# Loads in channel layout and stores as 128-partition transfers of 256 KB, in a fused transformer block on one NeuronCore

## The reference

```
x = x + conv_attention(ln_over_channels(x))      # q, k, v by 64x64 weights, 8 heads,
                                                 # softmax over an 8x8 score per head, Wout, bias
t = x as tokens (1024 x 64)
t = t + layer_norm(moe(ln(t)) + ln(t)) * gamma + beta
    # moe: routing weights from the mean token of an image, the best 2 of 8 experts,
    # each gelu(t W1 + b1) W2 + b2 with a hidden width of 128
out = t back as channels
```

## Time and profile before

| | us |
|---|---|
| median of 3 runs | 103.39 (103.19 to 103.40) |
| the profiled execution | 103.3 |
| its span, first to last instruction | 101.5 |
| TensorE busy | 86.3 |
| VectorE busy | 66.8 |
| ScalarE busy | 50.4 |
| GpSimd busy | 32.5 |

### The profile page before, as it was taken

One profiled execution on the slowest core, in us unless ns is written; L12 is line 12 of the kernel. 1 busy time (PEld: TensorE's weight loads), 2 busy tenths in 40 slices (PEclk: granted clock), 3 DMA queues, 4 the chain that ended last, 5 costly groups with the idle time before them and its releaser, 6 DMA issues.

```text
span 101.5 us, 2245 instructions
## 1 busy us (share of the span) xinstructions
PE 86.3 (85%) x748; PEld 45.9 (45%) x749; DVE 66.8 (66%) x235; ACT 50.4 (50%) x88; POOL 32.5 (32%) x82
## 2 busy tenths in 40 slices
PE   4997999997999978999869996899999999985200
PEld 1344796896751544699322272323423333341100
DVE  0098998964488998699999527261752726677920
ACT  0000765735666121138578998968877792510000
POOL 7000000008000000044380999472805601960500
PEclk9999999999999999999999999999999999999655
DMA  2999999800000000024200436830000260075075
GB/s 53 287 405 299 287 275 347 217 5 0 0 6 0 0 0 3 6 52 103 52 0 20 96 93 151 201 72 0 6 0 0 65 141 6 0 178 132 0 166 144
DMA packets 6554, 9.82 MB, mean 97 GB/s; under 512 B 1040, under 2 KB 3344, under 8 KB 6544
## 3 DMA queue, kind: packets, MB, share of 16 engines
q1 hardware_dynamic: 4848, 6.77, 25.4%
q10 hardware_dynamic: 1696, 2.92, 10.2%
HBM read 5.49 MB, written 2.10 MB: 75 GB/s over the span
## 4 chain that ended last, share of the span: by engine, by line
PE 69%; DVE 9%; DMA 7%; ACT 4%; issue 4%; ACTq 1%; DVEq 1%
PE pC L1221 14%; DMA cst<-consts_dram 7%; PE pB L917 4%; PE pS L917 4%; PE pA L927 4%; PE pA L1196 3%; PE pB L1196 3%; PE pM L1032 2%; PE pA L990 2%; PE pM L1004 2%; ACT SQ L433 2%; PE pC L1213 2%; PE pS L1066 2%; PE pC L978 2%; PE pS L978 2%
## 5 line engine op out<-in xcount | busy, mean ns | idle before, releaser
L1221 PE MATMUL pC<-H,w2g 128*64 128x512 f32 x64 | 15.8, 602 | 0.0
L484 POOL TENSOR_TENSOR LO<-UF,HI 128x512 f16<-128x512 f32 x8 | 9.2, 1159 | 20.4 <-ACT HI L344 19.5
L610 DVE BATCH_NORM_STATS2 bst<-XT 128x6 f32<-128x128 f32 x32 | 6.5, 282 | 4.9 <-DMA XT<-x_tok_dram 4.9
L1111 PE MATMUL pM<-wz 128*128 128x512 bf16 x25 | 8.0, 491 | 1.3 <-POOL wz L477 1.3
L238 POOL TENSOR_TENSOR XT<-XT,T 128x512 f32<-128x512 f32 x6 | 7.5, 1270 | 4.0 <-DVE XT L879 4.0
L420 ACT ACTIVATE H<-pA,b1s 128x1024 f32<-128x1024 f32 x6 | 6.7, 1111 | 2.5 <-PE pA L1196 2.3
L500 POOL COPY w1g<-w1hl 128x256 f16 x14 | 5.1, 402 | 8.1 <-issue 6.0
L344 ACT CAST HI<-UF 128x512 f16<-128x512 f32 x8 | 4.8, 618 | 5.1 <-DVE UF L718 5.1
L433 ACT ACTIVATE SQ<-pC,c 128x512 f32<-128x512 f32 x8 | 5.4, 686 | 3.8 <-PE pC L1221 3.0
L490 POOL TENSOR_TENSOR w1hl<-SQ,w1hl 128x512 f16<-128x512 f32 x2 | 2.3, 1156 | 15.2 <-DVE A L657 15.2
L855 DVE TENSOR_SCALAR U<-pC,c,wsm 128x512 f32<-128x512 f32 x8 | 6.2, 800 | 1.4 <-PE pC L1221 0.9
(11 more groups left out here) (230 smaller groups left out, 185.8 us busy)
## 6 DMA issues: line engine op xcount, KB each, us to landing
out_dram<-XT SPq DMA_DIRECT2D x14, 128.0 KB, 2.4
XT<-x_tok_dram SPq DMA_DIRECT2D x2, 512.0 KB, 8.9
X<-x_cha_dram SPq DMA_DIRECT2D x8, 128.0 KB, 11.0
X<-x_cha_dram ACTq DMA_DIRECT2D x8, 128.0 KB, 11.1
ST<-HI SPq DMA_DIRECT2D x6, 128.0 KB, 2.4
ST<-LO SPq DMA_DIRECT2D x6, 128.0 KB, 2.4
XT<-x_tok_dram SPq DMA_DIRECT2D x2, 256.0 KB, 4.6
XT<-x_tok_dram ACTq DMA_DIRECT2D x2, 256.0 KB, 4.8
```

Source lines behind the costliest of these rows:

```text
L484: nc.gpsimd.tensor_tensor(LO[:, p, cols], UF[:, p, cols], HI[:, p, cols], ALU.subtract).then_inc(s["lo"], 1)
L610: return nc.vector.bn_stats(bst[:, p, j, :], XT[:, p, j * P:(j + 1) * P].rearrange("p (b c) -> p c b", b=2))
L1111: mm(pM[:, :], wz[:, 0:P], wz[:, :], start=True, stop=True)
L1221: last = mm(half(y_ps[:, b * HALF:(b + 1) * HALF], h), w2g[:, p % 2, b, k, :], H[:, step % 2, b, h * HALF:(h + 1) * HALF], start=False, st ...
```

## The change

The loads of X and the stores of OUT now take both halves h of an image at once: one transfer of 128 partitions and 256 KB where there were two of 64 partitions and 128 KB. SP loads image 0 of each pair and ACT image 1. SP stores seven images, ACT the very last one; the store waits for one s_fin only. Each s_x[p] and s_out[p] now ends at 32. TensorE waits for cstb (s_cstb) before the experts' first products. No arithmetic is changed.

```
+        def both_halves(ap):
+            return ap.rearrange("c (h n) -> h c n", h=2)
+        def load_x(queue, p, b):
+            queue.dma_start(X[:, p, b * HALF:(b + 1) * HALF],
+                            both_halves(x_cha[b * C:(b + 1) * C, p, :])).then_inc(s_x[p], 16)
+        def store(queue, p, b):
+            queue.wait_ge(s_fin[2 * p + b], 1)
+            queue.dma_start(both_halves(out[b * C:(b + 1) * C, p, :]),
+                            OUT[:, p, b * HALF:(b + 1) * HALF]).then_inc(s_out[p], 16)
...
             for p in range(NP):
-                for b in range(2):
-                    sp.dma_start(X[0:C, p, b * HALF:(b + 1) * HALF],
-                                 x_cha[b * C:(b + 1) * C, p, 0:HALF]).then_inc(s_x[p], 16)
+                load_x(sp, p, 0)
...
             for p in range(NP):
-                for b in range(2):
-                    sp.wait_ge(s_fin[2 * p + b], 1)
-                    for h in range(2 if p < NP - 1 else 1):
-                        sp.dma_start(out[b * C:(b + 1) * C, p, h * HALF:(h + 1) * HALF],
-                                     OUT[h * C:(h + 1) * C, p, b * HALF:(b + 1) * HALF]).then_inc(s_out[p], 16)
+                for b in range(2 if p < NP - 1 else 1):
+                    store(sp, p, b)
             for p in range(NP):
-                sp.wait_ge(s_out[p], 64)
+                sp.wait_ge(s_out[p], 32)
...
             for p in range(NP):
-                for b in range(2):
-                    act.dma_start(X[C:P, p, b * HALF:(b + 1) * HALF],
-                                  x_cha[b * C:(b + 1) * C, p, HALF:N]).then_inc(s_x[p], 16)
+                load_x(act, p, 1)
...
-            for b in range(2):
-                act.wait_ge(s_fin[2 * NP - 2 + b], 1)
-                act.dma_start(out[b * C:(b + 1) * C, NP - 1, HALF:N],
-                              OUT[C:P, NP - 1, b * HALF:(b + 1) * HALF]).then_inc(s_out[NP - 1], 16)
+            store(act, NP - 1, 1)
...
-                dve.wait_ge(s_x[p], 64)
+                dve.wait_ge(s_x[p], 32)
...
             pe.wait_ge(s["w1h"], 2)
             pe.wait_ge(s["w1l"], 2)
+            pe.wait_ge(s_cstb, 16)
```

## The result

The changed kernel takes 149.87 us (median of 4 runs, 148.37 to 152.06), the kernel before 103.4 on the same chip. The ratio is 1.4364, with a 95% interval of 1.4326 to 1.4403. That is slower, by 45 us of 103, and inside the predicted range. The kernel was profiled twice. The profiled executions took 151.33 and 148.64 us, with spans of 149.5 and 146.8. Some executions take about 2% longer than the others, the first profiled one among them, and the ratio is that of the shorter ones (148.4 to 148.7 us).

The account below looks back on a forecast made before the run. Bound by TensorE and the VectorE and ScalarE steps it waits for, transfers only at the ends. Span 101.5 + 23.2 + 2.4 + 23.6 = 150.7, plus 1.8 and 0.1 gives 152.6 us; range 144 to 176.

Parts of the forecast that it names:

- Two engines: Changed X loads and stores: DRAM side 2x64x512 is dealt out by its first dimension, to two DMA engines instead of sixteen.
- Rival 1: Changed transfers: pattern is flattened, all sixteen engines carry them, the last store lands earlier; 102.3 us, chance 10%.
- The speed: Changed transfers: each DMA engine moves 24 GB/s, so 5.46 us a transfer; ends 25.9 and 14.9 to 16.3.
- rival 3: Changed transfers: two engines, packets as slow as in 64-partition rows; 200 us, some 176 with half that slowing; over 176: 8%.
- Term 1: X loads: last image pair lands at 56.3 us, so VectorE's last residual additions and everything behind move by +23.2 us.
- Rival 2: ScalarE's X issues: two engines, full queue holds ScalarE until 45.4; +34.6 in place of +23.2, 164.0 us, chance 13%.
- Term 2: TensorE after some 20 us waiting for X: restarts at the lower clock, +2.4 us, range 0 to 4.
- Term 3: Stores at the end: eight transfers of 5.46 us on the same two engines, one always waiting; +23.6 us.

## Why the prediction held, step by step

**Two engines: right.** The share of 0.12 at 48 GB/s that it named stands in both plateaus, at 0.13 and 50 to 51 GB/s (about 49 in the page's slices). With 16 and with 128 rows in front the share is 1.04, with four 0.27, so the engines follow the first dimension. Rival 1 (sixteen engines after all) is out for the changed kernel. As a statement on the kernel with 128 rows in front it was close, 102.3 against 101.6.

On the rule that the prediction had named for it (the Trainium skill, DMA: Bandwidth & Descriptors, section Why a DMA increments its semaphore by 16 and not by 1: the largest number up to 16 that divides the slowest dimension of both sides) the traces agree in all four cases: 2, 4, 16 and 16 engines.

**The speed: close.** Taken were 24 GB/s an engine and 5.46 us a transfer. The closing stretch of the second profile gives 51/2 = 25.5 GB/s for the stores, so 5.1 us. For the loads, the version with all of them on SP's queue shows a pair (two transfers) every 10.7 us, so 5.34 us a transfer and 24.5 GB/s an engine. The slow end of the range, 14.9 to 16.3, can be dropped for two engines, and with it rival 3.

**Term 1, the loads, +23.2: the size is right, the account of it only half.** Measured are +23.3 (33.13 to 56.44), and X is what released the last addition. The pairs' arrivals came out as well: 34.5, 45.4 and 56.3 were forecast, and VectorE read them at 35.0, 45.7 and 56.4 where nothing else held it. But the wait of some 20 us that VectorE was to have there is 1.49 and 2.45 in the two profiles. The delay had mostly come earlier, since ScalarE was held. Rival 2 had named that mechanism, and had set its end at 45.4, where the third of its transfers would have moved. The end was 32.6. The chain of waits of the second profile shows it (start, duration, what):

```profile
5.74 1.08 ACTq L239
6.85 3.69 ACTq L239
10.57 11.47 ACTq L239
22.07 34.29 DMA X<-x_cha_dram
```

The third issue takes 11.47 us and the fourth, from 22.07 to 32.60, 10.5, each about the 10.9 of a pair of transfers. They end at 22.1 and 32.6, just ahead of the 23.5 and 34.5 that the prediction gave for the first and second pair. So ScalarE's fourth issue ended with the second pair, not with the third, and the hold stayed 1.5 us short of deciding. That was in part luck: the forecast had left the hold out and given it to rival 2, and the hold happened to be just shorter than the delay of X itself. Both delays sat side by side, and the version without the hold showed that X alone makes all of term 1.

**Term 2, TensorE gone cold, +2.4: wrong in the shorter runs, and misplaced.** TensorE's long idle time lay at 20 to 40 us under the held ScalarE (4.96 us busy, clock 0.51), not ahead of the last pair. It cost almost nothing there: from ScalarE's first work to VectorE's addition of the first pair it is 50.29 - 32.60 = 17.7 us, against 28.29 - 10.83 = 17.5 before. By 40 to 55 us the clock was at 0.97 again. The price that was forecast does appear where the wait falls directly ahead of dense work: +2.5 in the first profile (clock 0.55 from 59 to 66) and +3.0 with all loads on SP's queue (0.50 from 57 to 66). So the size was about right where it was paid, and whether it was paid depended on the hold that term 1 had not counted. That the size fits is in part luck: it was taken from eleven weight loads at the program's head, where the granted clock reads 1.00, and not from a restart behind a wait.

**Term 3, the stores, +23.6: right, 1.5 too much.** The last part of the program is 44.4 us after the first issue, not 45.9. 2.10 MB at 51 GB/s are 41.1 us. With the 1.84 us from the issue to moving and 0.4 of closing that is 43.4. Of the 1.0 left over, the second profile shows two parts:

```profile
104.00:106.00 2.00, 1.88 (x20) 0.60 (x17) 0.92 (x2) 2.00 (x4) 0.00 (x0) 1.00 0.13 27
146.00:146.80 0.80, 0.00 (x0) 0.00 (x0) 0.00 (x0) 0.00 (x0) 0.00 (x0) 0.50 0.00 0
```

The burst starts at about half its later speed, 27 GB/s at the same share of 0.13, which by an estimate from these rows is worth some 0.4 us; and nothing moves after 146, so the closing is 0.8 us, not 0.4. No arithmetic was slowed, and nobody waited for a held SP.

**The sum.** 152.6, less 2.4 for the cold restart that the shorter runs don't have, less 1.5 for the stores, is 148.7. The profiled run took 148.64, and the lowest one 148.37. The median of 149.87 lies between these runs and the longer ones (150.88 to 152.06), of which the one with a profile, 151.33, pays the restart. In the chances there is a slip without consequence: the rivals leave 4% for an unchanged time and 86% for a slower one, and the prediction's closing line has 3% and 87%.

**What the change was meant to bring** is there once all engines are used: 1.8 us, against the 1.1 of rival 1 (103.4 - 102.3). It is all at the end. The larger store was no burden, since 128-partition stores ran at 385 GB/s in 97 to 98 us (share 1.02), and the 64-partition ones at 219 in 97 to 100 (share 0.92).

## What to carry to other kernels

Halving the number of transfers is worth a look at the first dimension of both sides, since in all four patterns tried here that number decided how many DMA engines worked: here the same 256 KB went at 50 GB/s with 2 in front and at 330 to 386 with 128. If two halves of the partitions come from different rows, lay the DRAM array out in the order of the partitions, or leave two transfers. And a slow transfer has two victims, its reader and the engine whose queue issues it; cost both before an edit frees one, because with the two nearly level the edit buys nothing.

## What the runs showed of the hardware beyond that

- **A queue pushes back on the engine that issues.** With sixteen engines an X issue took 0.6 us or 0.5 (four in 1.92 us in the version with 128 rows in front). With four engines four issues took 11.12 us, with two 26.83, and ScalarE does nothing else in that time. SP's four issues took 19.96 us in the same program and ended at 23.38, 9 us before ScalarE's. ScalarE's queue had the loads of w12 and cstb ahead of X, but no run tells whether that makes the difference.
- **The pattern matters among sixteen engines too.** 16x8 rows ran at 268 to 277 GB/s, 128 rows at 330 to 386, in the same stretches with all engines full, and the kernels differ by 1.1 us. No run here tells which rows each engine served, nor what the unused rows in DRAM do, so the cause stays open.
- **Stores on few engines don't keep one speed, and are slow at first.** On four engines they moved 45 and 29 GB/s when they began, later 102, and 76 in between, each time at a share of 0.24 to 0.26; on two engines 27, then 51, both at 0.13. Whether it comes from the stores themselves or from something beside them was not settled. It accounts for some 3 of the 8 us by which the kernel with four in front was missed, judged by 29.9 us of tail for the 26.9 that had been expected.
- **A short wait can be dearer than a long one.** Some 20 us of sparse TensorE work, followed by a sparse restart, cost 0.2 us. Waits for X of 2.45 us (first profile), 3.92 (4 in front, loads on SP) and 9.26 (two in front, loads on SP, the last of three such waits), right ahead of dense products, came with a clock of 0.55, of 0.67 to 0.79 and of 0.50 behind them, and cost 2.5, 1.1 and 3.0 us in these profiles; the waits of 1.49 in the second profile and of 2.12 with the loads alone came with 1.00 and cost nothing.
